# Layer 0 attention on TensorE: the second half of the transposed scores of groups 1 and 2 goes ahead of the value product

## What is computed

```python
Wdkv = x @ latent_w + latent_b
q = jnp.einsum('btc,hcl->bhtl', x, Wd_w) + Wd_b[None, :, None, :]
scores = jnp.einsum('bhtl,bsl->bhts', q, Wdkv) / sqrt(d_head)
scores = jnp.where(causal, scores, -jnp.inf)
attn = jax.nn.softmax(scores, axis=-1)
y = jnp.einsum('bhts,bsl->bhtl', attn, Wdkv)
return z @ out_w + out_b          # z is y with the heads side by side
```

## Time and profile before

| | |
|---|---|
| time, 3 runs | 1744.98, 1749.33, 1754.42 us (median 1749.33) |
| profiled execution, its own time | 1755.56 us |
| its span | 1753.8 us |
| mean granted TensorE clock | 0.955 |
| PE busy | 1529.9 us, 87% |
| DVE busy | 1158.3 us, 66% |
| ACT busy | 1010.6 us, 58% |
| POOL busy | 908.0 us, 52% |
| L1854, L1863, L1877, L1884 | 148.2, 85.8, 141.7, 82.1 us busy, 512 matmuls each |
| the chain that ended last | PE 66%, ACT 15%, DVE 5%, issue 5%, POOL 4%, DMA 2% |

### The profile page before, as it was taken

The page is one execution under the profiler, slowest core; times in us unless marked ns, Lnnn a source line. Parts: engine busy times, 40 slices in busy tenths (PEclk is TensorE's granted clock), DMA queues, the critical chain, the costliest instruction groups (busy, mean ns, idle before and its releaser), DMA issues.

```text
span 1753.8 us, 44847 instructions
## 1 busy us (share of the span) xinstructions
PE 1529.9 (87%) x13026; PEld 1081.8 (62%) x13027; DVE 1158.3 (66%) x4175; ACT 1010.6 (58%) x2526; POOL 908.0 (52%) x1625
## 2 busy tenths in 40 slices
PE   4799999999999999998999388888888888885882
PEld 4644555555555555545999377777777777764672
DVE  3437666666666666654555389889998998986661
ACT  3335555555555555554333478888888888862341
POOL 5224444444444444444443666666666666633663
PEclk9999999999999999999999699999999999996676
DMA  7403222222222222222332112121111212116444
GB/s 196 132 1 82 56 56 56 55 55 55 55 55 55 55 55 55 55 58 60 79 70 63 22 42 44 45 45 42 42 44 44 45 42 46 41 34 126 84 85 119
DMA packets 240883, 107.56 MB, mean 61 GB/s; under 512 B 145465, under 2 KB 229242, under 8 KB 240762
## 3 DMA queue, kind: packets, MB, share of 16 engines
q1 hardware_dynamic: 228410, 92.97, 22.4%
q0 software_dynamic: 10240, 13.64, 3.7%
q10 hardware_dynamic: 2176, 0.26, 0.1%
HBM read 61.92 MB, written 40.16 MB: 58 GB/s over the span
## 4 chain that ended last, share of the span: by engine, by line
PE 66%; ACT 15%; DVE 5%; issue 5%; POOL 4%; DMA 2%; SPq 1%; POOLq 0%; another core or an unknown queue 0%; DVEq 0%; ACTq 0%
PE bankA L1831 8%; PE bankT L1854 8%; PE bankB L1877 7%; PE bankT L1863 4%; PE bankB L1884 4%; PE bankT L2028 4%; PE bankB L1893 3%; ACT qx L1613 3%; ACT km L1622 2%; ACT gqx L1613 2%; PE bankT L2147 2%; PE bankA L2129 2%; ACT rows L1686 2%; PE bankT L2152 2%; DVE pt L1308 2%
## 5 line engine op out<-in xcount | busy, mean ns | idle before, releaser
L949 DVE CUSTOM_DVE_ANT_0 masked<-bankS,causal 128x128 bf16<-128x128 f32 x512 | 128.6, 288 | 237.2 <-PE bankS L1844 231.0
L653 POOL TENSOR_SCALAR_AFFINE_SELECT probs<-probs 128x512 f32<-128x512 f32 x256 | 160.3, 637 | 202.5 <-ACT probs L1510 148.4
L1499 ACT ACTIVATE qT<-bankA,bd 128x256 f32<-128x256 f32 x256 | 107.5, 471 | 194.7 <-PE bankA L1831 138.3
L952 DVE CUSTOM_DVE_ANT_0 masked<-bankS,causal 128x256 bf16<-128x256 f32 x512 | 195.6, 420 | 0.2
L1510 ACT ACTIVATE probs<-bankT 128x1024 f32<-128x1024 f32 x128 | 131.2, 1025 | 51.6 <-PE bankT L1854 48.8
L646 POOL CAST qb<-qT 128x256 bf16<-128x256 f32 x256 | 96.8, 399 | 119.0 <-ACT qT L1499 113.6
L1831 PE MATMUL bankA<-xnT,wd 128*128 128x256 f32 x512 | 153.7, 425 | 0.0
L1854 PE MATMUL bankT<-qT,kT 37*128 37x512 f32 x512 | 148.2, 656 | 0.8 <-ACT probs L1510 0.8
L1877 PE MATMUL bankB<-probs,vaug 128*64 128x512 f32 x512 | 141.7, 632 | 0.9 <-ACT yT L1518 0.9
L1308 DVE STREAM_TRANSPOSE pt<-pe 128x768 f32<-128x768 f32 x128 | 124.5, 972 | 25.4 <-ACT pe L1599 25.2
L2147 PE MATMUL bankT<-vx,pt 128*64 128x68 f32 x1024 | 72.9, 228 | 55.9 <-ACT gkm L1642 55.9
(11 more groups left out here) (314 smaller groups left out, 4197.4 us busy)
## 6 DMA issues: line engine op xcount, KB each, us to landing
rzb<-reciprocals SPq DMA_DIRECT2D x128, 128.0 KB
yT<-yT SPq DMA_DIRECT2D x64, 128.0 KB
xtab<-tab SPq DMA_DIRECT2D x32, 192.0 KB, 2.0
xs_sorted<-zeros SPq DMA_DIRECT2D x1, 4608.0 KB, 19.2
qT<-xs_sorted SPq DMA_DIRECT2D x144, 32.0 KB, 1.7
ys_sorted<-qT SPq DMA_DIRECT2D x36, 128.0 KB, 1.9
value_rows<-vrow SPq DMA_DIRECT2D x32, 128.0 KB, 1.8
vx<-value_rows SPq DMA_DIRECT2D x256, 16.0 KB, 1.8
```

The lines of the kernel that those rows point to most:

```text
L653: pool.affine_select(out=blocks, in_=blocks, compare_op=ALU.is_ge, fill=0.0, base=0, pattern=[[0, 4], [1, P]], channel_multiplier=-1).then ...
L949: dve.tensor_tensor_reduce(masked[:, e, 0:P], bankS[:, e, 0:P], causal[:, P:2 * P], -1.0, -NEG, ALU.add, ALU.min, mneg[:, n.half, e, j, 0:1])
L952: ins = dve.tensor_tensor_reduce(masked[:, e, P:3 * P], bankS[:, e, P:3 * P], causal[:, :], -1.0, -NEG, ALU.add, ALU.min, mneg[:, n.half, ...
```

## The change

In groups 1 and 2 of each step, `st_second` moves from between the two halves of the value product to the front of them. Nothing is added or removed, on any engine.

```diff
                 st_first(b, 1, True)
                 if n:
                     smax(n, 2)
+                st_second(b, 1, True)
                 av_first(b, 0, "ranks" if ranks else q is not None)
-                st_second(b, 1, True)
                 av_second(b, 0)
                 if n:
                     smax(n, 3)
@@
                 st_first(b, 2, True)
                 if n:
                     smax(n, 4)
+                st_second(b, 2, True)
                 av_first(b, 1, True)
-                st_second(b, 2, True)
                 av_second(b, 1)
```

## The result

| | before | after |
|---|---|---|
| runs | 4 | 4 |
| median | 1751.7 us | 1723.81 us |
| lowest to highest | 1744.98 to 1754.42 | 1723.06 to 1727.32 |
| ratio | | 0.985, 95% interval 0.9817 to 0.9884 |
| profiled execution | 1755.56 us | 1727.32 us |

The kernel became faster by 1.5%, 27.9 us by the medians, where 22.5 were forecast. The time lies in the range of 1720 to 1740, the gain is 5.4 us larger than its forecast. The interval leaves out 1, so the change is clear of the noise.

The account below looks back on a forecast made before the run. PE alone was taken to bound the attention. Savings of 20.2 (loop), 1.4 (steps 30 and 31), 0.9 (step 0) and 0 (step 1) sum to 22.5 us, taking the median from 1749.3 to 1726.8 us; range 1720 to 1740.

Parts of the forecast that it names:

- PE alone sets the pace: Attention of layer 0: PE is busy for all of 500.00 us, so shortening its stream shortens the kernel equally.
- The sum per group, 0.36: Groups 1 and 2: L1844 to the next smax takes 2.07 us instead of 2.43, saving 0.36 per group.
- stand-in row: Starts taken from rows of the same products or forms elsewhere: 0.11, 0.52, 0.91 and 0.53 us.
- the first rival: Weights of L1863 not in time in the loop: 0.15 us saved per group, 9 us, time 1740; chance 0.09 with other partial gains.
- The sum of the three upper bounds: Per group, with all three pessimistic terms: 2.35 us, saving only 0.08.
- Drain and open load as two parts: Each change between split rows and split columns costs about 0.1 us before it and about 0.1 behind it.
- the second rival: No gain: weight loads are hidden in either order, so the order would not matter; time 1749, chance 0.05.
- Steps 30 and 31, and the loop: Loop steps 2 to 29 save 20.2 us over 56 groups; four groups in steps 30 and 31 save 1.4.
- Steps 0 and 1: Step 0, at half clock, saves 0.9 us; step 1 saves nothing because PE waits for DVE's maxima.
- Who becomes late: The next smax, waiting for DVE's reduction, is tightest with 0.26 us of room; the moved L1863 has 1.1 us for ACT.
- The size, 27.9 us for 22.5: Whole kernel: 22.5 us saved, to a median of 1726.8 us; chance 0.81.

Follow-up runs that it names:

- scores_behind: Against the kernel before, the second scores moved behind the second value product in groups 1 and 2; 1731.16 us, ratio 0.9922.
- again_before: The unchanged kernel before, profiled a second time; first L1893 at 147.0 us, then 661.2 us on to the first L2017.

## Why the prediction was right

*PE alone sets the pace.* Right: busy 500.00 of 500.00 us after as before, and the step shrinks by what PE's stream shrinks.

*The sum per group, 0.36.* It measured 0.35: 0.11 + 0.53 + 0.91 + 0.53 = 2.08 us for 2.07 forecast, in both groups of a step of the loop. Each stand-in row named the right number, the one from the written-out code too: the register computation ahead of L1863 in the loop costs nothing. That was the first rival, and it fell with the loads at 498.14. The sum of the three upper bounds was miscounted: 0.21 + 0.63 + 0.91 + 0.58 is 2.33 and would have saved 0.10, not 2.35 and 0.08. Nothing else rests on it.

*Drain and open load as two parts.* Right for the sum, since each term came from a row. The general price, 0.1 us before a change of form and 0.1 behind it, is too round: two changes fewer would save 0.40. The 0.1 before a change was there each time. Behind it L1863 lost 0.10 us, L1884 0.05, and an `smax` 0.01 at most (0.07 us from L1842 to L1844 for 0.06). The reading of the earlier trace rows that all four loads start with the matmul holds for the first two. The Trainium skill's rule (TensorEngine Tiling (Array Packing), Key Properties) of a drain at each change of mode agrees with the rows, 0.10 us more ahead of each change, but alone it would have given 12 us. scores_behind shows the part that hangs on the loads of L1863, 0.10 us per group. The Trainium skill's other rule, that PE pulls weight loads ahead (TensorE: Matmul & The Clock Gate, Step-by-step), is seen in this case only between products of one form, as at 498.14, and not at 498.78. So the second rival, by which the order would not matter, fell too.

*Steps 30 and 31, and the loop: 20.2 + 1.4 = 21.6 us.* Measured 21.5, of which the loop has 19.6.

*Steps 0 and 1: 0.9 us.* This term was wrong. It measured nothing: the first L1893 is at 148.1 to 148.5 us after, and at 148.1 or 148.2 in the middle of the six before. Step 0 does get shorter: the L1820 at its end comes at 121.08 to 121.49 us, and at 122.33 to 123.50 in four of the six before. Part of that goes with the rise of the clock, which came a little earlier there. But step 1 gives it back. From that L1820 to the first L1893 it takes 26.98 us after and 24.69 in again_before. Of the 2.3 us more, the stretch at half clock is 1.64, and the rest are longer waits for DVE, which also swallow what the two groups save. The prediction had the waits and not the clock.

*Who becomes late.* The spacing of `smax` to `smax` in groups 1 and 2 is 2.14 us after the change (498.08 to 500.22), and the least is 1.88, so the 0.26 us of room was real and is left. Three experiments used it up, and in each the spacing stopped at 1.87 or 1.88 us.

*The size, 27.9 us for 22.5.* The stages that the change touches save 21.5 us, and the rest behind the attention takes 932 to 938 us in both. So some 6 us of the 27.9 lie outside those stages, by these profiles. The first profile of before shows where such time can come from: 8 us at its start and 4.5 behind the loop, in events that the profiles of the changed kernel happen not to have. How often the runs without a profile had them can't be seen. The medians of before in the later comparisons were 1751.02 and 1746.63 us, those of after 1723.81 and 1724.03. Over all executions of the two kernels, 28 of before and 9 of after, the means are 1748.7 and 1724.0 us, 24.7 apart. So a part of the 27.9 is the scatter of the first few runs, and the forecast of 22.5 is nearer to the truth than the first result shows, though one of its terms, the 0.9 of the start, came to nothing. Whether the old order meets these events more often stays open; six profiles of it against three don't settle it.

## What to carry to other kernels

Where TensorE is busy without a gap, read its timeline from start to start: the same product cost half as much again here (0.63 for 0.43 us) when both its neighbours split the array in another way, and putting the products of one form together took 0.35 us off each group with no other edit. Count the changes of form per step before and after, price one from rows of this kernel, and price a hidden weight load by itself. Then measure the least spacing of the loop between TensorE and the engine behind it (here 1.88 us from `smax` to `smax`), because each product that is taken out from between two of them uses that room up.

## What the runs showed of the hardware

- A product of 37 rows x 256 columns for both halves of the rows takes 0.43 us between its own kind (484.85 to 485.28 in the changed kernel), 0.53 on one side of a change between split rows and split columns (498.25 to 498.78), and 0.63 with a change on both sides (518.29 to 518.92 before).
- Behind a bf16 `smax` on the same split of the rows, the first loads of the 32-bit weights of the next product start 0.11 us ahead of it (498.14 for 498.25), though from the first start of the `smax` to the next product only 0.17 us go by (498.08 to 498.25). Behind a value product they start with it (505.11 in scores_behind), and the product takes 0.10 us longer than its 0.43.
- A stretch of some 3.4 us at the half level of the clock (granted clock 0.53 from 141 to 144 us) stood right behind a wait of PE of 1.19 us, with work at the full level before and after. It came at this place in all three profiles of one order of the instructions and in none of the eleven of others, so it seems tied to the order, by what is open. A longer one (0.50 from 784 to 790 us) stood behind a wait of 1.78 us in one profile of the kernel before.
